# A fused scan-and-feed-forward kernel: the order of its opening stretch rewritten

## What is computed

```python
x = x + attn(layernorm(x)); x = x + ffn(layernorm(x))
# attn:
proj = x @ in_proj_w.T                  # gate 8192, xBC 8192 + 2*8*128, dt 128
xBC  = silu(conv4(xBC) + conv_b)        # 4 taps along time, one filter per channel
dt   = softplus(dt + dt_bias); cum = cumsum(dt * A) within a chunk
scores  = (C_i . B_j) * exp(cum_i - cum_j) * dt_j    # lower triangle
y_intra = scores @ x;  y_inter = (C * exp(cum)) @ state
state   = exp(cum_last) * state + (dt * exp(cum_last - cum) * B)^T x
g = (y_intra + y_inter + D * x) * silu(gate)
out = (g * rsqrt(mean(g*g) per group + eps) * norm_w) @ out_w.T
# ffn: w2(silu(w1 x) * (w3 x)), each product with its LoRA term
```

## Time and profile before

| | us |
|---|---|
| median of 3 runs (1740.88 to 1742.11) | 1740.98 |
| profiled execution | 1740.52 |
| its span | 1738.7 |
| PE busy | 1726.2 (99%) |
| DVE busy | 1224.0 (70%) |
| ACT busy | 1193.6 (69%) |
| POOL busy | 1182.1 (68%) |
| DMA moved | 211.63 MB, mean 122 GB/s |

### The profile page before, as it was taken

How to read it: one execution, slowest core, us unless ns; L and a number is a source line. 1 busy time by engine, 2 the same in 40 slices (tenths; PEclk the granted TensorE clock), 3 DMA queues, 4 the chain that set the end, 5 groups by cost and what they waited for, 6 DMA issues and landing times.

```text
span 1738.7 us, 27749 instructions
## 1 busy us (share of the span) xinstructions
PE 1726.2 (99%) x9932; PEld 1437.7 (83%) x9932; DVE 1224.0 (70%) x2154; ACT 1193.6 (69%) x2233; POOL 1182.1 (68%) x1058
## 2 busy tenths in 40 slices
PE   8999999999999999999999999999999999999999
PEld 6788888888888888888888888888888888887887
DVE  8896678758785768677876878576867688663323
ACT  6877677777867677767777786767777777763421
POOL 5586768676777668676868677766867686874510
PEclk9999999999999999999999999999999999999999
DMA  4734445344544444343534454344444353344201
GB/s 148 215 105 113 128 111 172 95 120 116 164 121 115 118 145 111 116 125 116 168 109 114 109 161 128 114 121 146 111 120 115 112 174 104 114 116 134 80 15 49
DMA packets 122056, 211.63 MB, mean 122 GB/s; under 512 B 24256, under 2 KB 28992, under 8 KB 121920
## 3 DMA queue, kind: packets, MB, share of 16 engines
q1 hardware_dynamic: 121920, 209.87, 41.7%
HBM read 205.09 MB, written 4.72 MB: 121 GB/s over the span
## 4 chain that ended last, share of the span: by engine, by line
PE 96%; DVE 2%; ACT 1%; DMA 0%; issue 0%; POOL 0%; SPq 0%; DVEq 0%
PE bank L1690 18%; PE bank L1692 18%; PE bank L1691 18%; PE bank L1766 7%; PE bank L1824 7%; PE bank L1807 7%; PE bank L1814 7%; PE bank L1781 5%; PE bank L1740 2%; PE bank L2069 1%; PE bank L2068 1%; PE bank L2070 1%; PE bank L1840 1%; PE bank L1750 1%; PE bank L1931 1%
## 5 line engine op out<-in xcount | busy, mean ns | idle before, releaser
L698 POOL TENSOR_TENSOR w_l<-w_raw,w_h 128x512 fp32r<-128x512 f32 x288 | 380.4, 1324 | 341.4 <-ACT w_h L893 341.4
L1690 PE MATMUL bank<-x_h,w_h 128*128 128x512 f32 (+1 forms) x1328 | 526.2, 396 | 1.4 <-DVE bcT L1366 1.3
L1692 PE MATMUL bank<-x_h,w_l 128*128 128x512 f32 (+1 forms) x1328 | 519.1, 391 | 0.0
L1691 PE MATMUL bank<-x_l,w_h 128*128 128x512 f32 (+1 forms) x1328 | 517.4, 390 | 0.0
L1366 DVE SCALAR_TENSOR_TENSOR x_ch<-bank,par,x_ch 128x511 f32<-128x511 f32 (+2 forms) x384 | 287.1, 749 | 82.3 <-ACT x_ch L911 73.3
L946 ACT ACTIVATE decay<-decay,cols 128x128 f32<-128x128 f32 x1024 | 318.3, 390 | 1.7 <-POOL decay L704 0.9
L1692 PEld LDWEIGHTS bank<-x_h,w_l 128*128 128x128 f32 (+1 forms) x1328 | 248.8, 187 | 54.4
L1690 PEld LDWEIGHTS bank<-x_h,w_h 128*128 128x128 f32 (+1 forms) x1328 | 249.2, 188 | 52.2 <-POOL w_l L698 2.2
L1691 PEld LDWEIGHTS bank<-x_l,w_h 128*128 128x128 f32 (+1 forms) x1328 | 249.4, 188 | 51.1
L1396 DVE TENSOR_TENSOR decay<-decay,bank 128x512 f32<-128x512 f32 x256 | 171.4, 682 | 107.5 <-ACT decay L946 107.5
L911 ACT ACTIVATE x_ch<-bank,par 128x512 f32<-128x512 f32 x128 | 99.1, 774 | 186.7 <-PE bank L1692 186.7
(11 more groups left out here) (162 smaller groups left out, 2768.1 us busy)
## 6 DMA issues: line engine op xcount, KB each, us to landing
w_raw<-in_wp SPq DMA_DIRECT2D x288, 256.0 KB, 3.2
decay<-cum_scratch SPq DMA_DIRECT2D x256, 256.0 KB, 4.0
ec<-ecum_scratch SPq DMA_DIRECT2D x96, 256.0 KB, 6.3
ow_raw<-in_ow SPq DMA_DIRECT2D x64, 256.0 KB, 4.6
w_raw<-in_w SPq DMA_DIRECT2D x48, 256.0 KB, 2.7
acc<-in_x SPq DMA_DIRECT2D x8, 256.0 KB, 4.5
out<-acc SPq DMA_DIRECT2D x8, 256.0 KB, 2.0
cols<-cols_scratch SPq DMA_DIRECT2D x16, 96.0 KB, 2.7
```

What stands on the lines that cost most here:

```text
L698: pool.tensor_tensor(w_l[:, s, :], w_raw[:, s, :], w_h[:, s, :].bitcast(F32), ALU.subtract).then_inc(wl_ready, 1)
L1690: pe.matmul(dst, wh, xh, start=(opens and k == 0), stop=False)
L1691: pe.matmul(dst, wh, xl, start=False, stop=False)
L1692: last = pe.matmul(dst, wl, xh, start=False, stop=(k == len(terms) - 1 and not more))
```

## The change

- Layer norm: on DVE the statistics of chunks 2 and 3 come before the normed rows of chunks 1 to 3, and statistics of later chunks move likewise. SP loads all four chunks of sequence 0 ahead of the two small inputs, whose first use on ACT (`a_pos`) moves behind two weight casts. POOL's remainder of the dt weights waits for the four normed chunks.
- `warm` issues matmuls of 512 columns in place of transposes of 128, 8, 4 and 2 of them (14) where there were 13 and four times 2 (21).
- The transposes of chunk 4 move behind the first tile, the later ones a tile further; `step_product(1)` now stands behind 5 tiles where it stood behind 4.
- `turn_cols` stands behind tiles 6 and 12 (5 and 10 before), `match` behind 16 (15), and on ACT the first `exps` at tile 8 (9), with `decayed(1)` behind the second of them and no longer ahead of the first. DVE's `copy_cols(0)` moves behind the taps of the next convolution tile, and tile ("c", 2) gets its taps ahead of `step_sums(1)`.
- Tile 0 of the second unit is projected ahead of `turn_x` of the first chunk, and tile 1 ahead of `inside`; so the first scan step has one tile fewer behind it. On DVE `scale_x` moves ahead of `scores`, `gated` ahead of `add_state`, the taps of the second unit's tile 2 right behind it. SP's refills move with them.

The diff, cut to its core:

```diff
-TURN_AT = (5, 10)
-MATCH_AT = 15
-EXP_AT = 9
-MASK_AT = 12
-WARM = (13, 2, 2, 2, 2)
+TURN_AT = (6, 12)
+MATCH_AT = 16
+EXP_AT = 8
+MASK_AT = 11
+WARM = (8, 4, 0, 0, 2)
...
             for c in range(CHUNKS):
                 sp.dma_start(acc[:, c, :], x_t[c]).then_inc(x_loaded[c], 16)
-                if c == 1:
+                if c == SC - 1:
+                    sp.dma_start(wdt_raw, wdt_in).then_inc(wdt_loaded, 16)
+                if c == SC:
                     sp.dma_start(a_log[:, :], a_log_in).then_inc(small_loaded, 16)
                     sp.dma_start(dt_bias[:, :], dt_bias_in).then_inc(small_loaded, 16)
-                if c == SC - 1:
-                    sp.dma_start(wdt_raw, wdt_in).then_inc(wdt_loaded, 16)
...
-            refill(TURN_AT[0])
+            refill(5)
+            refill(6)
             store_cols(0, range(KINDS))
-            refill(TURN_AT[0] + 1)
...
             pool.wait_ge(wdt_h_ready, 1)
+            pool.wait_ge(xn_ready, SC)
...
             for n in range(LEAD + TILES):
+                w_low(0, n // TILES, n % TILES)
                 if n < SC:
                     norm_inverse(0, SC + n)
-                if n == LEAD + TILES - 2:
-                    weigh_x(0, 0)
-                    xw_low(0, 0)
-                w_low(0, n // TILES, n % TILES)
...
+            weigh_x(0, 0)
+            xw_low(0, 0)
...
-                if i == 3:
+                if i == 4:
+                    decayed(0)
                     absolute(1)
                     exponential(1)
-                    decayed(0)
...
-                if i == EXP_AT - 1:
-                    decayed(1)
                 if EXP_AT <= i < EXP_AT + QUARTERS:
                     exps(0, 0, i - EXP_AT)
+                if i == EXP_AT + 1:
+                    decayed(1)
...
             norm_moments(0, 0)
-            for i in range(1, SC):
-                norm_moments(0, i)
-                norm_apply(0, i - 1)
-            norm_apply(0, SC - 1)
+            norm_moments(0, 1)
+            norm_apply(0, 0)
+            norm_moments(0, 2)
+            norm_moments(0, 3)
+            norm_apply(0, 1)
+            norm_apply(0, 2)
+            norm_apply(0, 3)
...
                 if FIRST_ORDER[i] == ("c", 0):
                     step_log(1)
+                if FIRST_ORDER[i] == ("c", 1):
                     copy_cols(0)
-                if FIRST_ORDER[i] == ("c", 1):
                     step_size(1)
+                if FIRST_ORDER[i] == ("c", 2):
                     step_sums(1)
...
+            scale_x(0, 0)
             for q in range(QUARTERS):
                 scores(0, 0, q)
-            scale_x(0, 0)
...
                     if first:
+                        gated(g, k)
                         for j in range(OW_EARLY // 2):
                             ow_low(g, j)
-                    add_state(g, k)
...
+                        add_state(g, k)
+                        taps_of(tiles[2:3])
...
                 for _ in range(n):
-                    pe.transpose(ob[:, 0:P], ident[:, :], ident[:, :])
+                    pe.matmul(ob[:, :], ident_r[:, :], ident_r[:, :].unsqueeze(1).broadcast_to([P, KT, P]), start=True, stop=True)
...
             step_product(0)
-            norm_transpose(0, SC)
...
                 project(0, 0, i)
-                if i < 3:
-                    norm_transpose(0, SC + 1 + i)
-                if i == 3:
+                if i < SC:
+                    norm_transpose(0, SC + i)
+                if i == SC:
                     step_product(1)
...
+            project(0, 1, 0)
             pe.wait_ge(cols_out, KINDS * BATCH)
             turn_x(0, 0)
...
                     if first:
-                        projects(tiles[:1])
+                        projects(tiles[1:2])
                     inside(g, k)
                     if first:
-                        projects(tiles[1:2])
+                        projects(tiles[2:3])
...
                     new_state(g, k)
                     if first:
-                        projects(tiles[2:3])
+                        projects(tiles[3:4])
```

More of the change, by code:

```diff
@@ L558, in _ @@
             store_cdec(1)
-            for i in range(10, 13):
+            for i in range(10, 14):
                 refill(i)
             store_cols(1, range(KINDS))
+            refill(14)
             load_ow(0, range(OW_EARLY))
+            for i in range(15, TILES - 1):
+                refill(i)
             sp.wait_ge(cdec_stored, 16 * BATCH)
@@ L565, in _ @@
                 sp.wait_ge(cols_stored[n], 32 if n < 2 else 16)
-            for i in range(13, TILES - 1):
-                refill(i)
             sp.wait_ge(rows_stored, 16 * BATCH)
@@ L632, in body @@
                             load_next_w(g - 1, False, 1, TILES - 1)
+                            load_ow(g, range(OW_EARLY, OW_EARLY + 2))
                         else:
                             refill(TILES - 1)
-                        load_ow(g, range(OW_EARLY, OW_EARLY + 2))
+                            load_next_w(g, last, b, tiles[0])
+                            load_ow(g, range(OW_EARLY, OW_EARLY + 2))
+                            load_next_w(g, last, b, tiles[1])
                     if more:
@@ L647, in body @@
                         load_next_w(g, last, b, tiles[0] - 1)
-                    for i in tiles[:1]:
-                        load_next_w(g, last, b, i)
+                    first = not some(K)
+                    if not first:
+                        load_next_w(g, last, b, tiles[0])
                     if k == 0:
                         load_ow(g, range(OW_EARLY + 2, CT))
-                    for i in tiles[1:-1]:
+                    for i in tiles[2 if first else 1:-1]:
                         load_next_w(g, last, b, i)
@@ L1199, in body @@
                     first = not some(g * CHUNKS + k)
-                    tile(tiles[:1])
                     if first:
-                        for j in range(OW_EARLY // 2, OW_EARLY):
-                            ow_high(g, j)
+                        w_high(*ahead(g, b, tiles[0], LEAD))
                         tile(tiles[1:2])
+                    else:
+                        tile(tiles[:1])
                     gT_high(g, k)
@@ L1208, in body @@
                         tile(tiles[2:3])
+                        for j in range(OW_EARLY // 2, OW_EARLY):
+                            ow_high(g, j)
                     copy_b(gn, kn)
@@ L1226, in body @@
                     exps(gn, kn, 2)
-                    tile(tiles[3:-1])
+                    if not first:
+                        tile(tiles[3:-1])
                     exps(gn, kn, 3)
+                    if first:
+                        tile(tiles[3:-1])
                     silus()
@@ L1653, in body @@
                         scores(gn, kn, 1)
-                    taps_of(tiles[2:3])
+                    if not first:
+                        taps_of(tiles[2:3])
                     if k == 0:
@@ L2036, in body @@
                     out_half(g, k, 0)
-                    projects(tiles[3:-1])
+                    if not first:
+                        projects(tiles[3:-1])
                     if k == 0:
```

60 lines of the change are left out of this document (30 added, 30 removed).

## The result

| | us |
|---|---|
| median before (20 runs, 1740.13 to 1742.33) | 1741.20 |
| median after (20 runs, 1742.27 to 1745.45) | 1744.12 |
| ratio after to before, 95% interval | 1.0015 [1.0009, 1.0021] |
| profiled execution after, its span | 1744.44, 1742.7 |

The change makes the kernel slower by 0.15%. That is less than the 0.2% that the prediction calls telling, but it is surely not a gain. The forecast was 1736.0 with a range of 1732.8 to 1739.0: the time is outside it, on the other side of the kernel before.

A forecast was written before the change was run, and what follows sets the result against it. PE, busy 99%, bounds the kernel, so only its losses in the head count: 4.1 + 0.75 + 0.8 - 1.9 + 1.3 = 5.05, say 5.0, off 1740.52 gives 1735.5, median 1736.0; range 1732.8 to 1739.0.

The forecast's parts named there:

- Start of the dt product and full clock: First dt product on PE: starts at 11.0, not 12.67, and takes 2.8, not 5.2; gain 4.1.
- rival (b): Clock rises no sooner than the first dt product, whose twelve matmuls take 5.2 again; 2.6 gained, 1738.4; chance 0.14.
- Second dt product: Standing a tile later, it finds x_l of the last chunk ready; 3.54 becomes 2.8, gain 0.75.
- Before `turn_x`: PE's wait of 0.83 for the last silu is covered by tile 0 of the next unit; gain 0.8.
- Columns: Second `turn_cols` waits for read-back columns landing at 52.3 and starts at 57.0, not 55.1; loss 1.9.
- its 3.75: Gain forecast for the head, the part ahead of `inside` in the first scan step.
- First scan step: From `inside` to the second `new_state`: the wait of 1.33 for tile 2's taps goes; gain 1.3.
- the bound: First scan step's lower bound: four `ow_low` pairs stretched beside POOL make DVE 2 late, a loss of 1.2.
- the better value: Gain of 1.3 taken for the first scan step, in place of the loss of 1.2 with stretched pairs.
- Later on: From 200 us to the end: PE waits about 1 as before, so only the head moves the time.
- the sign: Observation in the trace after that would show the sum wrong: a DVE wait before the output product's second half.

The follow-up runs named there:

- e8: Kernel after with the old order of norm statistics for chunks 1 to 3 and the old narrow transposes at the start; 1746.06, ratio to before 1.0032.
- e3: Kernel after with 22 zero-weight products, 512 columns wide, filling PE's wait for the low output weights in the first scan step; 1742.15, ratio to before 1.0006.
- e11: Kernel before with POOL waiting in the first scan step until DVE has made all eight low output weights; 1740.94, ratio 1.0000.
- e4: Kernel after with POOL waiting in the first scan step until DVE has made all eight low output weights; 1739.48, ratio to before 0.9991.
- e1: Kernel before with the new start alone: changed order of loads, statistics and rows of x, and wide first products; 1740.08, ratio 0.9993.
- e5: Kernel after with one second-unit tile on PE moved from ahead of `inside` to behind the output product's first half; 1745.32, ratio to before 1.0021.
- e7: e6 with `fade` also moved behind the last pair, and POOL's `xw_low` ahead of `w_low`; 1743.37, ratio to before 1.0010.
- e6: Kernel after with DVE's last `ow_low` pair behind the next scores, its four products behind the second `new_state`; 1742.62, ratio to before 1.0005.

## Why the prediction was wrong

- **Start of the dt product and full clock, +4.1: right in size.** 11.07 and 2.86 long against 11.0 and 2.8. Its clock part, 2.0, reaches `turn_x` whole (e8). With wide products the first dt product runs at the full pace in nine traces of ten, and rival (b) is seen in one, e3. With the narrow transposes it runs at half pace in all three (before, e8, e11). The reading that the clock doesn't rise on narrow transposes holds for the kernel before alone: in e8 the norm transposes at 5.89 and 7.15 take 0.37 from start to start for four, against 0.55 at 5.84 in the kernel before, and the pace is low again at 9.68, with 0.50 in the window of 9 to 10; e11 has 0.38 at 7.91 and 0.55 at 11.37. There the clock rose and fell back.
- **Second dt product, +0.75: right.** It takes 32.18 - 29.41 = 2.8, without a wait before its third part.
- **Before `turn_x`, +0.8: right.** No wait, 75.98.
- **Columns, -1.9: mechanism right, size near.** `turn_cols` starts at 57.86 behind a wait for `cdecT`, where 57.0 was predicted; this is what the head is short of its 3.75. The `exps` start at 53.03, not at 52.3. That was partly luck: DVE copied the columns at 41.20, not 1.3 sooner than before but 0.2 later, and the first store went out at 41.91 and not at 40.3, but the last piece landed early in the range given. The wait is 0.72 only, because PE had already lost 1.42 for taps of x, which no step named: ACT stood 2.51 for a weight load, its logarithm came late and DVE was idle for it. Together 2.1 for 1.9.
- **First scan step, +1.3: this step failed.** The 1.3 itself came, as no wait for the taps is left behind the first half of the output product. What failed is the price of DVE's queue: the forecast had nothing for it, and its sentence on the bound, "with four stretched pairs DVE would be 2 late at the second half of the output product, a loss of 1.2", had too little. DVE's queue could be added up from the trace of before: from `scale_x` to the end of the last pair there are 14.7 of operations besides the pairs, all of durations that the kernel before shows too. With pairs of 1.41 they end at 76.9 + 20.3 = 97.2, ahead of PE (98.9); with pairs of 3.98 at 107.5, 8.6 behind it. The measured 12.4 for the pairs, and a fade of 2.32 for 1.65, give 104.4 and the wait of 5.4. The bound was too small by more than 6, because only PE's missing cover was priced and not the sum of the queue. The reason given for the better value turned against it: "`gated` moved ahead pulls ACT's and POOL's chain (gT, masks, xw) forward by some 4 us" came true, POOL's `xw_l` starts at 101.09 instead of 105.03, but there it runs beside the last pair, which was over at 102.7 before. e4, which holds back just these operations of POOL, gets 4.6 back.
- **The clock in that wait: in no term.** The text treats the clock at the start alone. Behind the wait of 5.4 PE ran at 0.50 for more than 5 us, another 2.3 by e3.
- **Later on:** the prediction had PE wait about 1 as before; it is 0.8 more than before. Right but for that.

At the second `new_state` the two come to 5.4 + 2.7 (1.0 for the `ow_l` products, 1.7 for `inside`) = 8.1, and it is 8.0 late; without them the sum would have held. That is in part luck: the 0.7 that the head is short was made up by two short waits of the old step, 0.3 and 0.39 before its state products, which are gone. The prediction did name the sign: the sum would be wrong "if a wait for DVE stood before the output product's second half".

## What to carry to other kernels

When a tile of PE work is moved ahead of a step, it is taken from the cover of that step: add up the queue of the next-busiest engine through the step, with its stretched durations, and compare its end with PE's new arrival. Take a gain at the start through every fixed chain behind it before it is counted (here DVE's queue of normed rows and running sums, which took most of it in e1). When a chain on a third engine is pulled forward, look at what it will then run beside. A wait long enough to drop PE's clock costs twice.

## What the runs showed of the hardware

- PE's granted clock fell to 0.50 in a wait of 5.4 and was there in the windows from 104 to 110, with PE at work again. It stayed at 1.00 through a wait of 2.32 in e4; behind one of 2.33 in e5 the windows of 78 to 80 and 80 to 82 show 0.78 and 0.50, and the 32 products of `inside` took 3.5. In e7 a wait of 3.35 ended at 109.27, and the windows of 108 to 110 and 110 to 112 show 0.89 and 0.50: the fall came as the wait ended and cost the work behind it.
- At the start, one wait of 1.47 behind eight and four wide products was followed by 0.50 in e3, and one of 1.38 in e4 was not: the same instructions, two outcomes.
- Behind 13 narrow transposes PE ran at the full pace in e8 (5.9 to 8.4) and was at 0.50 from 9 to 15; in the kernel before, with the same transposes, it ran at half pace from 5.8 on while the column of the granted clock says 1.00.
- A pair of `ow_low` takes 1.40 alone (e4) and up to 4.7 beside POOL (e3, e6, e7), while the taps, which read PSUM, keep their 2.30.
